# TensorE leaves out every wait for a semaphore value that it has already waited for

## What is computed

```
for each chunk of 128 tokens:
    out  = (silu(q W0) * (q W2)) W1                  # read with the weights so far
    dW   = gradient(k, v, lr) + M * momentum;  M = dW
    X    = dW / ||dW||_F
    for a, b, c in NS_COEFFS:                         # 5 times
        A = X X^T;  B = b A + c A A;  X = a X + B X
    W    = renorm(W + X)
y = x + layernorm((ttt_out + attention) Wo)
z = y + layernorm(gelu(layernorm(y) P1^T + b1) P2^T + b2)
```

## Time and profile before

| | |
|---|---|
| median of 3 runs | 379.28 us (378.91 to 379.86) |
| the profiled execution | 379.39 us |
| its span, from the first to the last instruction | 377.6 us |
| mean granted TensorE clock | 0.997 |
| PE busy | 369.0 us (98%) |
| PEld / DVE / ACT / POOL busy | 294.4 / 256.9 / 212.1 / 193.9 us |
| the chain that ended last | PE 88%, DVE 5%, POOL 2%, ACT 2%, issue 2% |

### The profile page before, as it was taken

How to read it: one execution, slowest core, us unless ns; L and a number is a source line. 1 busy time by engine, 2 the same in 40 slices (tenths; PEclk the granted TensorE clock), 3 DMA queues, 4 the chain that set the end, 5 groups by cost and what they waited for, 6 DMA issues and landing times.

```text
span 377.6 us, 15942 instructions
## 1 busy us (share of the span) xinstructions
PE 369.0 (98%) x6754; PEld 294.4 (78%) x6754; DVE 256.9 (68%) x676; ACT 212.1 (56%) x429; POOL 193.9 (51%) x289
## 2 busy tenths in 40 slices
PE   8989999999999999999999999999999999999994
PEld 7577788756888878878577888689887757988883
DVE  4688998582478699898547746987875492767124
ACT  2889865756603765649733446665357575614500
POOL 5499666354248656485963524364333440557211
PEclk9999999999999999999999999999999999999998
DMA  7652100002000000000000200000000110000101
GB/s 261 241 176 88 43 2 5 3 3 59 3 3 2 3 2 3 4 4 3 17 17 17 71 16 3 2 2 17 19 4 4 40 37 2 0 3 0 57 0 56
DMA packets 9685, 12.22 MB, mean 32 GB/s; under 512 B 912, under 2 KB 8720, under 8 KB 9616
## 3 DMA queue, kind: packets, MB, share of 16 engines
q1 hardware_dynamic: 9616, 11.22, 9.1%
HBM read 9.12 MB, written 2.10 MB: 30 GB/s over the span
## 4 chain that ended last, share of the span: by engine, by line
PE 88%; DVE 5%; POOL 2%; issue 2%; ACT 2%; POOLq 0%; DVEq 0%; ACTq 0%
PE pair L776 15%; PE pair L787 15%; PE pair L553 7%; PE pair L695 6%; PE pair L685 6%; PE pair L707 6%; PE pair L676 5%; PE pair L757 3%; PE pair L562 3%; PE pair L585 3%; PE pair L726 3%; PE pair L742 3%; PE pair L656 2%; PE pair L733 2%; PE pair L623 1%
## 5 line engine op out<-in xcount | busy, mean ns | idle before, releaser
L776 PE MATMUL pair<-xn2T,p1T 128*128 128x512 f32 (+1 forms) x160 | 59.1, 512 | 0.0
L787 PE MATMUL pair<-p2T,h 128*128 128x256 f32 x256 | 57.0, 379 | 0.0
L787 PEld LDWEIGHTS pair<-p2T,h 128*128 128x128 f32 x256 | 48.0, 190 | 6.4 <-issue 0.2
L1408 POOL TENSOR_SCALAR var<-mv 128x1 f32<-128x1 f32 (+1 forms) x54 | 13.0, 242 | 63.6 <-DVE mv L1363 35.0
L1029 ACT ACTIVATE h<-pair,packed_in 128x512 f32<-128x512 f32 (+1 forms) x40 | 23.9, 602 | 36.1 <-PE pair L776 36.1
L776 PEld LDWEIGHTS pair<-xn2T,p1T 128*128 128x128 f32 x160 | 28.7, 190 | 17.1 <-issue 14.7
L1403 POOL TENSOR_TENSOR nq<-ssq,half 128x8 f32<-128x8 f32 (+1 forms) x16 | 24.2, 1512 | 26.5 <-DVE ssq L1135 26.5
L1051 DVE SCALAR_TENSOR_TENSOR A<-pair,eye 128x512 f32<-128x512 f32 x45 | 28.8, 683 | 13.0 <-PE pair L685 12.7
L1403 POOL TENSOR_TENSOR rstd<-var,neg_half 128x1 f32<-128x1 f32 (+1 forms) x55 | 33.4, 607 | 7.1 <-DVE var L1366 2.5
L1051 DVE SCALAR_TENSOR_TENSOR B<-pair,eye 128x512 f32<-128x512 f32 x45 | 28.9, 684 | 10.0 <-PE pair L695 9.9
L982 ACT ACTIVATE masked<-masked,nmax 128x256 f32<-128x256 f32 (+1 forms) x32 | 15.1, 472 | 26.6 <-DVE nmax L1292 26.6
(11 more groups left out here) (165 smaller groups left out, 771.6 us busy)
## 6 DMA issues: line engine op xcount, KB each, us to landing
x_in<-in_L_attn_x_dram SPq DMA_DIRECT2D x16, 128.0 KB, 2.5
x<-in_L_attn_x_dram SPq DMA_DIRECT2D x16, 128.0 KB, 2.1
out_dram<-rows_a SPq DMA_DIRECT2D x16, 128.0 KB, 1.7
p1T<-in_L_ffn_proj_dram SPq DMA_DIRECT2D x1, 1024.0 KB, 5.0
p2T<-in_L_ffn_proj_dram SPq DMA_DIRECT2D x1, 1024.0 KB, 7.5
W<-in_states_dram SPq DMA_DIRECT2D x1, 768.0 KB, 6.7
wqkv<-in_Wall_dram SPq DMA_DIRECT2D x1, 512.0 KB, 3.9
WT<-in_states_dram SPq DMA_DIRECT2D x1, 512.0 KB, 6.4
```

The source lines that it names most:

```text
L776: mm_ = pe.matmul(ps[:, at], p1T[:, k, n * P:(n + 1) * P], xn2T[:, k, at], start=(k == 0), stop=(k == KC - 1))
L787: mm_ = pe.matmul(ps[:, 0:DIM], h[:, n, b * P:(b + 1) * P], p2T[:, n, :], start=(n == 0), stop=(n == HC - 1))
```

## The change

On PE every wait goes through an `Unmet` object, which keeps the highest value waited for on each semaphore and issues nothing when a new wait asks for no more than that. `take_pair` merges the waits of its two banks into the higher one when both are of one signal. What each step computes, the bank plan, the order of the matmuls and all other engines stay as they are.

```diff
+class Unmet:
+
+    def __init__(self, eng):
+        self.eng, self.met = eng, {}
+
+    def wait_ge(self, signal, n):
+        if n > self.met.get(signal, 0):
+            self.met[signal] = n
+            self.eng.wait_ge(signal, n)
...
                 last = free(bank, signal, c, n)
                 if last is not None:
-                    pe.wait_ge(*last)
+                    unmet.wait_ge(*last)
                 return BANK[bank]
...
                 one, other = free(bank, signal, c, n), free(bank + 1, signal, c, n)
+                if one is not None and other is not None and one[0] is other[0]:
+                    one, other = (one[0], max(one[1], other[1])), None
                 if one is not None:
-                    pe.wait_ge(*one)
-                if other is not None and other != one:
-                    pe.wait_ge(*other)
+                    unmet.wait_ge(*one)
+                if other is not None:
+                    unmet.wait_ge(*other)
...
             def NB(bank, c, it, g):
                 take_pair(bank[0], "B", c, 3 * it + g + 1)
-                pe.wait_ge(*S["A"](c, 3 * it + g + 1))
+                unmet.wait_ge(*S["A"](c, 3 * it + g + 1))
...
```

More of the change, by code:

```diff
@@ L497, in _ @@
         def _(pe):
+            unmet = Unmet(pe)
             owner = {}
@@ L524, in XT_ @@
                     ps = take(bank[0], "first_xnT", 0, b + 1)
-                    pe.wait_ge(*S["first_xn"](0, b + 1))
+                    unmet.wait_ge(*S["first_xn"](0, b + 1))
                     for k in range(KC):
@@ L532, in XT_ @@
                     return
-                pe.wait_ge(*S["xn"](c, 1))
+                unmet.wait_ge(*S["xn"](c, 1))
                 for k in range(KC):
@@ L541, in MM @@
                 ps = take(bank[0], "mm", c, 1)
-                pe.wait_ge(*S["ms"](c, 1))
+                unmet.wait_ge(*S["ms"](c, 1))
                 for i in range(2):
@@ L548, in QK @@
             def QK(bank, c, b):
-                pe.wait_ge(ld_qkv, 16)
+                unmet.wait_ge(ld_qkv, 16)
                 ps = take(bank[0], "qk_raw", c, b + 1)
-                pe.wait_ge(*(S["xnT"](c, 2) if c else S["first_xnT"](0, b + 1)))
+                unmet.wait_ge(*(S["xnT"](c, 2) if c else S["first_xnT"](0, b + 1)))
                 for k in range(KC):
@@ L556, in VV @@
             def VV(bank, c, b):
-                pe.wait_ge(ld_v, 16)
+                unmet.wait_ge(ld_v, 16)
                 ps = take(bank[0], "v_raw", c, b + 1)
-                pe.wait_ge(*(S["xnT"](c, 2) if c else S["first_xnT"](0, b + 1)))
+                unmet.wait_ge(*(S["xnT"](c, 2) if c else S["first_xnT"](0, b + 1)))
                 for k in range(KC):
@@ L569, in TR @@
                     ps = take(bank[0], "att_T", c, u + 1)
-                    pe.wait_ge(*S["qk_raw"](c, 4))
+                    unmet.wait_ge(*S["qk_raw"](c, 4))
                 else:
                     ps = take(bank[0], "ttt_T", c, u - 3)
-                    pe.wait_ge(*(S["qn"](c, 4) if c else S["silu"](0, 4) if u < 6 else S["qn"](0, u - 5)))
+                    unmet.wait_ge(*(S["qn"](c, 4) if c else S["silu"](0, 4) if u < 6 else S["qn"](0, u - 5)))
                 for b in range(BATCH):
@@ L603, in DH @@
                 take_pair(bank[0], "dh", c, 1)
-                pe.wait_ge(*S["ttt_T"](c, 6 if c else 2))
-                pe.wait_ge(*(S["W"](c, 1) if c else (ld_w, 16)))
+                unmet.wait_ge(*S["ttt_T"](c, 6 if c else 2))
+                unmet.wait_ge(*(S["W"](c, 1) if c else (ld_w, 16)))
                 for b in range(BATCH):
@@ L630, in OUT @@
                     take_pair(bank[0], "yg", c, 1)
-                pe.wait_ge(*S["gT"](c, bp + 1))
+                unmet.wait_ge(*S["gT"](c, bp + 1))
                 for y_ in range(2):
@@ L646, in DW @@
                         if g == 0:
-                            pe.wait_ge(*S["klv"](c, 4))
-                    pe.wait_ge(*S[ready](c, bp + 1))
+                            unmet.wait_ge(*S["klv"](c, 4))
+                    unmet.wait_ge(*S[ready](c, bp + 1))
                     for y_ in range(2):
@@ L664, in SS @@
                 if c == 0 and g == 0:
-                    pe.wait_ge(prepared, 1)
-                pe.wait_ge(*S["mom_ss"](c, g + 1))
+                    unmet.wait_ge(prepared, 1)
+                unmet.wait_ge(*S["mom_ss"](c, g + 1))
                 pe.matmul(ps[:, 0:8], ones_blk[:, :], m_ss[:, g, :], start=True, stop=True).then_inc(S["ss_ps"].sem, 1)
@@ L671, in TX @@
                 if it == 0:
-                    pe.wait_ge(*S["x0"](c, g + 1))
+                    unmet.wait_ge(*S["x0"](c, g + 1))
                 else:
-                    pe.wait_ge(*S["X"](c, 3 * (it - 1) + g + 1))
+                    unmet.wait_ge(*S["X"](c, 3 * (it - 1) + g + 1))
                 for b in range(BATCH):
@@ L680, in NA @@
                 take_pair(bank[0], "A", c, 3 * it + g + 1)
-                pe.wait_ge(*S["XT"](c, 3 * it + g + 1))
+                unmet.wait_ge(*S["XT"](c, 3 * it + g + 1))
                 for n in range(4):
@@ L702, in NX @@
                 take_pair(bank[0], *done)
-                pe.wait_ge(*S["B"](c, 3 * it + g + 1))
+                unmet.wait_ge(*S["B"](c, 3 * it + g + 1))
                 for n in range(4):
@@ L714, in WX @@
                 ps = take(bank[0], "WT", c, g + 1)
-                pe.wait_ge(*S["W"](c, g + 1))
+                unmet.wait_ge(*S["W"](c, g + 1))
                 for b in range(BATCH):
@@ L723, in SC @@
                 if b == 0:
-                    pe.wait_ge(*S["att_T"](c, 4))
+                    unmet.wait_ge(*S["att_T"](c, 4))
                 for hd in range(NAH):
@@ L730, in PT @@
                 ps = take(bank[0], "pT", c, b + 1)
-                pe.wait_ge(*S["prob"](c, b + 1))
+                unmet.wait_ge(*S["prob"](c, b + 1))
                 for n in range(4) if c else (1, 3):
@@ L737, in PV @@
                 ps = take(bank[0], "comb", c, b + 1)
-                pe.wait_ge(*S["pT"](c, b + 1))
+                unmet.wait_ge(*S["pT"](c, b + 1))
                 for hd in range(NAH):
@@ L746, in CT @@
                 ps = take(bank[0], "cT", c, b + 1)
-                pe.wait_ge(*S["comb"](c, b + 1))
+                unmet.wait_ge(*S["comb"](c, b + 1))
                 for k in range(KC):
@@ L752, in WO @@
             def WO(bank, c, b):
-                pe.wait_ge(ld_wo, 16)
+                unmet.wait_ge(ld_wo, 16)
                 ps = take(bank[0], "wo_n", c, b + 1)
-                pe.wait_ge(*S["cT"](c, b + 1))
+                unmet.wait_ge(*S["cT"](c, b + 1))
                 for k in range(KC):
@@ L761, in NT @@
                 ps = take(bank[0], "xn2T", c, b + 1)
-                pe.wait_ge(*S["xn2"](c, b + 1))
+                unmet.wait_ge(*S["xn2"](c, b + 1))
                 for k in range(KC):
@@ L771, in F1 @@
                 if c == 0 and n == 0:
-                    pe.wait_ge(ld_p1, 16)
+                    unmet.wait_ge(ld_p1, 16)
                 if n == 0:
-                    pe.wait_ge(*S["xn2T"](c, 2 if part == 0 else 4))
+                    unmet.wait_ge(*S["xn2T"](c, 2 if part == 0 else 4))
                 for k in range(KC):
@@ L782, in F2 @@
                 if c == 0 and b == 0:
-                    pe.wait_ge(ld_p2, 16)
+                    unmet.wait_ge(ld_p2, 16)
                 if new:
-                    pe.wait_ge(*S["h"](c, HC if b == 0 else 2 * HC))
+                    unmet.wait_ge(*S["h"](c, HC if b == 0 else 2 * HC))
                 for n in range(HC):
@@ L798, in run @@
                         parts[kind](PLAN[step], c, *arg)
-            pe.wait_ge(warm, 1)
+            unmet.wait_ge(warm, 1)
             for n in range(9):
                 pe.matmul(BANK[7][:, (n % 4) * P:(n % 4 + 1) * P], ones[:, :], ones[:, :], start=True, stop=True)
-            pe.wait_ge(consts, 1)
+            unmet.wait_ge(consts, 1)
             run(ORDER)
```

8 lines of the change are left out of this document (4 added, 4 removed).

## The result

The changed kernel is slower. Its median is 381.2 us (380.15 to 383.38, 11 runs) against 379.11 us for the kernel before (378.8 to 379.86, 11 runs); the ratio is 1.0051, with a 95% interval of 1.0035 to 1.0067. The forecast was 378.6 us with a range up to 379.6. The spread is also new: 3.2 us from the lowest to the highest run, where it was 1.1.

A forecast was written before the change was run, and what follows sets the result against it. PE was taken as the bound nearly everywhere. Eight earlier starts sum to 0.72 us, taking the kernel's own 379.39 us to 378.67; the median lies 0.11 lower, so 378.6 us, range 377.7 to 379.6.

The forecast's parts named there:

- a separate wait that is already met costs nothing: PE's list: the sequencer handles met waits while PE works through earlier instructions; only unmet waits count; size nothing.
- Met waits removed: no cost and no gain: PE's list, 294 instructions less: leaving out met waits changes the time by nothing, covered by PE's queued work.
- D: Whole kernel slower, 380.4 us, with hand-overs through a carried wait above 0.04 us as its sign; chance 6%.
- Unmet waits that become carried: PE's late starts after copies: hand-over 0.04 instead of 0.14 us, gaining at most 0.10 us each.
- The sum of 0.72 us: Eight places along the chain, from 9.7 to 285.0 us, where PE starts earlier, gaining 0.05 to 0.10 us each.
- the NX steps at 96.5 and 259.9 us: Two NX stretches where PE starts late: gains of 0.08 us at the first and 0.10 at the second.
- Rival A: All late hand-overs: the whole loss comes back, 1.1 to 1.5 us, about 377.9 us; chance 15%.
- B: PE's removed met waits each give back part of their 51 ns: 1 to 3 us, 377.3 us; chance 5%.
- C: Each lead of PE is used up by the next copy, so nothing reaches the end: 379.2 us; chance 12%.
- What would show it: Signs: 15,648 instructions, issue near 254 and 284 us falling from 0.14 to 0.04, 1.56 us stretches unchanged.
- the 1.7 us of NX: Three NX steps near 259 us still take some 1.7 us, not 1.56, as the sign that DVE's pace sets them.

The follow-up runs named there:

- the order alone: Kernel before, each PE matmul asking for its unmet wait first, all 407 separate waits kept; 378.97 us, ratio 0.9995.
- 96 and 128: Changed kernel plus 96 separate met waits in the F2 steps of chunk 0 and 128 in those of chunk 1; 378.9 us, ratio 1.0006.
- experiment 6: Kernel before plus 960 small matmuls, 3840 PE instructions, ahead of its first step, waiting for nothing; 438.95 us.

## Why the prediction was wrong

**The step that failed** is the first: "a separate wait that is already met costs nothing [...] the number of waits is the wrong thing to count". In the sum it is the term "Met waits removed: no cost and no gain": it was put at nothing, and it measured 2.5 us of stops. The half on the sequencer's time held for this kernel, where at most a few waits stand ahead of a matmul: the three NX or NB steps of a stretch still take 1.56 us where nothing stops them (260.22, NB, 1.56 us), and in the trace of the kernel before 342 separate waits are recorded while 1 to 19 weight loads ahead of them in the list have yet to start. What I had not counted is that each wait is also 64 bytes of PE's instruction stream (16,384 bytes to 256 records). Their number sets where the block ends fall, and a block end in a dense stretch cost up to 1.5 us in the kernels of this study. My sum had no term for PE's instructions at all, although the page's q8 row and the 16,384-byte packets were there in the profile before. None of the rivals held it either; D, the one on the slower side, was about the carried waits.

**Unmet waits that become carried:** the hand-over of 0.04 us is right (at 256.03 and 286.92). The traces give the parts of the first of them, the TX step that takes x0 from DVE. In the kernel before DVE's signal comes at 254.103 us, the separate wait is recorded from 254.132 to 254.183, the weight load starts at 254.208 and the matmul at 254.238; in that trace no load behind a separate wait starts sooner than 24 ns after the wait's record has ended. In the changed kernel the signal comes at 256.028 and the load, which carries the wait, starts at 256.070. The sum of 0.72 us is what the order alone shows in the profiled execution (376.9 against 377.6 us), but not by the forecast's terms one by one: with the order alone the NX steps at 96.5 and 259.9 us gave nothing (in the changed kernel 0.08 and 0.09), and 0.18 us came between 287 and 289 us, where the forecast had none and where the kernel before passes the block end 11968 (below). In the medians only 0.2 us of the sum is seen, in this kernel and in the one with 96 and 128, and both intervals include no change. So a gain of 0.72 us in the time is not shown.

**Rival A** (all of the loss comes back): no, the NX steps at 260 us still take 1.77 us. **B** (removed waits give back their own time): its price of 51 ns was the record's length, where one wait after another takes 0.106 us; behind an unmet separate wait a Newton-Schulz step starts its first four loads within 49 ns (three cases in the kernel before), where behind a carried one 20 ns are usual, but both have started 17 loads after 0.23 us; and removed waits give nothing back here: the kernel with all 407 separate waits in another order is no slower than the kernel with 96 and 128 (378.97 and 378.9 us), and the stretches of 1.56 us stay 1.56. **C** (nothing reaches the end): not in the traces, since with the order alone the lead is there at the end of the span; the medians can't exclude it. **D** (slower, since a release through a carried wait takes longer): no, 0.04 us. How many matmuls stand ready behind a carried wait no run shows; what the traces show is that no separate wait is recorded with more than 19 loads ahead of it still to start.

**What would show it:** the issue at the hand-overs, 15,648 instructions and the 1.7 us of NX came as the forecast said, and the time was still wrong. Signs that confirm each term don't confirm that the terms are complete.

**Why the kernel before had no stops:** its list ends its blocks at harmless places, and this isn't robust. PE passes number 11712 at 283.55 us, 1.31 us after its packet has landed, and 11968 at 287.69 us, 1.44 us after it, the same as at the end of a stop: nothing was to spare there. Moving its list on by 96 instructions costs 5.3 us. Whether some change elsewhere had been kept because it happened to place the blocks well, no run here can show.

**Open:** when in a block the next one is asked for (the start times of q8's packets don't fit one instruction number), what passes in the 1.2 to 1.6 us between a packet's landing and PE's start, why the packet ahead of 12224 comes late in two kernels, and how much of a run's spread of 1 to 3 us is due to the time that a packet takes (0.88 to 1.75 us in all traces).

## What to carry to other kernels

Where PE goes through more than one block of 256 instructions in 3.5 to 4 us (3.45 to 4.00 a block in the added stretch of experiment 6), its instruction stream is a resource of its own (no run here tests another engine), and any edit that adds or removes instructions, however free they look, moves the block ends. Look for idle time with "issue" in the middle of a step, count the instructions up to it, and see whether the numbers agree modulo 256 and whether each stop ends 1.2 to 1.6 us after an instruction packet has landed; then try the same edit with some met waits added ahead of the dense part before it is judged. Of two waits ahead of a matmul, ask first for the one that is not yet met: PE then started 0.04 us after the copy's end instead of 0.14.

## What the runs showed of the hardware

- In the added stretch of small matmuls PE's instructions came at one block of 16,384 bytes in 3.45 us at best; such matmuls with their loads use one up in 2.09 us.
- PE starts on a block no sooner than 1.21 us after its packet has landed (650 block ends), and each of 31 stops ended 1.21 to 1.59 us after it.
- Each of the 33 stops of over 0.2 us at a late block, in eight kernels of this study, stands 192 instructions over a multiple of 256 of PE's list.
- Under other DMA traffic two blocks came later: standstills of 3.51 and 4.65 us at DMA shares of 0.89 and 0.98, against 1.36 us at 0.01. It was the start of the packet that was late.
- Separate waits that follow each other start 0.106 us apart in the median (153 pairs), though the record of one shows 51 ns. Three ahead of a matmul of 0.43 us were covered, eight were not: from the first to the 64th record of the F2 steps of chunk 0 it is 22.28 us in the kernel before, 22.32 with 96 waits more and 36.22 with 256.
